# A two-layer kernel whose state-space chunks are computed one pipeline slot further ahead, beside a feed-forward network

## What is computed

```python
# branch 1: state space layer (4 heads of 64, state of 128), 2048 tokens
h   = h * dA_t[:, :, None, None] + dtx_t[..., None] * B_t[:, :, None, :]   # per token, a scan
y_t = einsum('bhpn,bhn->bhp', h, C_t)
y   = (y + D * xh) * silu(z);   out = residual + einsum('bli,di->bld', y, out_proj_w)
# branch 2: feed-forward network of ternary weights, width 512
h = silu(_tlin(x, w1_w, w1_s)) * _tlin(x, w2_w, w2_s)
h = gelu(_tlin(h, h1_w, h1_s));  h = gelu(_tlin(h, h2_w, h2_s));  out = _tlin(h, w3_w, w3_s)
```

## Time and profile before

| | |
|---|---|
| time of three runs | 628.39 us median (627.77 to 628.84) |
| the profiled execution: its own time | 632.69 us |
| its span of instructions | 630.9 us |
| mean granted clock of PE | 0.984 of full speed |
| busy over the span: PE, PEld, DVE, ACT, POOL | 582.4, 345.5, 371.0, 453.5, 142.8 us |

### The profile page before, as it was taken

How to read it: one execution, slowest core, us unless ns; L and a number is a source line. 1 busy time by engine, 2 the same in 40 slices (tenths; PEclk the granted TensorE clock), 3 DMA queues, 4 the chain that set the end, 5 groups by cost and what they waited for, 6 DMA issues and landing times.

```text
span 630.9 us, 11320 instructions
## 1 busy us (share of the span) xinstructions
PE 582.4 (92%) x4048; PEld 345.5 (55%) x4053; DVE 371.0 (59%) x1022; ACT 453.5 (72%) x602; POOL 142.8 (23%) x171
## 2 busy tenths in 40 slices
PE   4669999999999999999897899799989999999998
PEld 4324334444343333333334477478767888888887
DVE  7884765646444353475516765683276676676753
ACT  2368988999989999989666275555766576566663
POOL 2043222020110011002700745103003131222231
PEclk9878999999999999999989999999999999999999
DMA  7112002013422220210317220200000000000000
GB/s 229 29 34 68 2 1 68 1 41 105 169 96 92 101 85 1 69 68 9 109 26 224 67 73 39 80 2 0 0 1 1 2 18 0 1 18 1 2 17 18
DMA packets 31175, 31.00 MB, mean 49 GB/s; under 512 B 6912, under 2 KB 21024, under 8 KB 31120
## 3 DMA queue, kind: packets, MB, share of 16 engines
q1 hardware_dynamic: 29872, 27.71, 14.0%
q0 software_dynamic: 1248, 2.57, 1.1%
HBM read 13.44 MB, written 12.89 MB: 42 GB/s over the span
## 4 chain that ended last, share of the span: by engine, by line
PE 64%; DVE 19%; ACT 7%; issue 5%; POOL 2%; SPq 1%; DMA 1%; DVEq 0%; POOLq 0%; ACTq 0%
PE ps L1311 18%; PE ps L1292 9%; PE ps L92 4%; PE ps L94 4%; PE ps L93 4%; PE ps L1622 2%; PE ps L1388 2%; PE ps L1375 2%; DVE r L2449 1%; PE ps L1488 1%; PE ps L1204 1%; DVE r L2388 1%; ACT r L958 1%; DVE r L2385 1%; SPq L706 1%
## 5 line engine op out<-in xcount | busy, mean ns | idle before, releaser
L958 ACT ACTIVATE r<-ps 128x1024 f32<-128x1024 f32 x272 | 258.4, 1034 | 34.2 <-PE ps L1292 31.7
L1311 PE MATMUL ps<-r 128*32 128x512 f32 (+3 forms) x1280 | 147.9, 549 | 2.2 <-DVE r L2043 1.0
L835 POOL TENSOR_SCALAR_AFFINE_SELECT r<-r 128x512 f32<-128x512 f32 (+1 forms) x80 | 47.8, 602 | 218.7 <-ACT r L958 218.4
L1292 PE MATMUL ps<-r2r 32*128 32x512 f32 (+3 forms) x640 | 79.3, 452 | 8.1 <-DMA r2r<-r2r 4.3
L1292 PEld LDWEIGHTS ps<-r2r 32*128 32x128 f32 x640 | 34.8, 186 | 51.4 <-ACT r L958 20.8
L873 POOL TENSOR_TENSOR r<-r 128x512 f32<-128x512 f32 x16 | 23.1, 1446 | 139.0 <-ACT r L1129 139.0
L1311 PEld LDWEIGHTS ps<-r 128*32 128x32 f32 x1280 | 28.0, 109 | 42.7 <-issue 30.3
L94 PE MATMUL ps<-r2r 128*128 128x512 f32 x112 | 44.3, 395 | 0.0
L93 PE MATMUL ps<-r2r 128*128 128x512 f32 (+1 forms) x96 | 35.8, 372 | 0.0
L813 POOL DMA_INDIRECT rows_by_expert<-r x16 | 17.8, 1110 | 63.2 <-DVE r L1958 59.4
L1129 ACT ACTIVATE r<-r 128x512 f32<-128x512 f32 x16 | 10.1, 633 | 28.7 <-DVE r L2449 28.7
(11 more groups left out here) (405 smaller groups left out, 1208.5 us busy)
## 6 DMA issues: line engine op xcount, KB each, us to landing
rows_by_expert<-r SPq DMA_DIRECT2D x34, 258.0 KB, 2.5
r2r<-r2r SPq DMA_DIRECT2D x60, 64.0 KB, 2.0
r<-in_f_W SPq DMA_DIRECT2D x1, 2048.0 KB, 9.3
r<-rows_by_expert SPq DMA_DIRECT2D x23, 64.5 KB, 1.8
res<-in_x SPq DMA_DIRECT2D x4, 256.0 KB, 4.1
r<-in_g_h1T SPq DMA_DIRECT2D x1, 1024.0 KB, 5.7
r<-in_g_h2T SPq DMA_DIRECT2D x1, 1024.0 KB, 7.9
r<-rows_by_token SPq DMA_DIRECT2D x4, 256.0 KB, 3.9
```

Source lines behind the costliest of these rows:

```text
L835: pool.affine_select(blk, blk, pattern, ALU.is_ge, nothing, base=0, channel_multiplier=-1).then_inc(s_msk, 1)
L958: act.activation(probs[:, n % PBUFS, :, :], ps[:, b:b + 2, :], ACT.Exp).then_inc(s_exp, 1)
L1292: m = pe.matmul(ps[:, 2 * (n % SBUFS) + h, at:at + TB - query], kst[32 * j:32 * j + 32, group, P * kt:P * kt + P], qst[32 * j:32 * j + 32, ...
L1311: m = pe.matmul(ps[32 * j:32 * j + 32, 6, query:TB], vp[:, kt, group, :], probs[:, (2 * v + j // 2) % PBUFS, j % 2, at:at + TB - query], s ...
```

## The change

`chunk(i + 1)` on PE moves from the odd slot, behind `state(i)`, to the even slot 2i, behind `projected(i - 1)` and ahead of `state(i)`. On DVE `chunk_started(i + 1)` moves from the even slot 2i + 2 to the odd slot 2i + 1, behind that slot's low half and `chunk_added`; `weighted` stays in the even slot, behind `state_carried`. On ACT the exponentials move from ahead of the gelu of the even slot to behind the gelu (and behind the tanh) of the odd slot before it. A semaphore `s_cb` counts `dtx`, the last reader of the product bank on DVE, and stands in for two waits: PE's on the operands of DVE ahead of `chunk(i)`, and DVE's on its own steps in `weighted`. The work itself, its sizes and its instructions are the same.

```diff
@@ ACT
                 for o in range(FO):
                     if o == 0:
                         gated_high(b, FO - 1)
-                    if o % 2 == 0:
-                        decays(SLOT(b, o) // 2)
+                        if not b:
+                            decays(0)
                     middle_gelu(b, o)
+                    if o % 2:
+                        decays(SLOT(b, o) // 2 + 1)
                 for o in range(FO):
                     if o and b < NB - 1:
                         gated_high(b + 1, o - 1)
-                    if o % 2 == 0:
-                        decays(SLOT(b, FO + o) // 2)
                     last_gelu(b, o)
                     if b < NB - 1:
                         up_tanh(b + 1, o)
+                    if o % 2 and SLOT(b, FO + o) // 2 + 1 < NCH:
+                        decays(SLOT(b, FO + o) // 2 + 1)
@@ PE
             def chunk(i):
                 if i:
-                    pe.wait_ge(s_cx, 2 * i)
+                    pe.wait_ge(s_cb, i)
                     pe.wait_ge(s_ce, 2 * i)
...
             def chunk_units(s):
                 if s % 2:
                     state(s // 2)
+                else:
+                    if s:
+                        projected(s // 2 - 1)
                     if s // 2 + 1 < NCH:
                         chunk(s // 2 + 1)
-                elif s:
-                    projected(s // 2 - 1)
@@ DVE
-                step.mark(dve.tensor_tensor(dtx[:, b], ps[:, 0, P:P + DI].rearrange("p (h d) -> p h d", h=NH),
-                                            over(dt_f[:, NH * i:NH * i + NH], PD), ALU.mult))
+                dve.tensor_tensor(dtx[:, b], ps[:, 0, P:P + DI].rearrange("p (h d) -> p h d", h=NH),
+                                  over(dt_f[:, NH * i:NH * i + NH], PD), ALU.mult).then_inc(s_cb, 1)
             def weighted(i):
                 b = i % 2
-                step.settle()
+                dve.wait_ge(s_cb, i + 1)
...
-                    if s % 2:
+                    if s == 0:
+                        chunk_started(0)
+                        weighted(0)
+                    elif s % 2 == 0:
+                        state_carried(s // 2 - 1)
+                        weighted(s // 2)
+                        if o == 0:
+                            down_added(b - 1)
+                    else:
                         if s >= 3:
                             chunk_added(s // 2 - 1)
                         if o == 1 and b:
                             finished(b - 1)
-                    elif o == 0:
-                        chunk_started(s // 2)
-                        if b:
-                            state_carried(s // 2 - 1)
-                        weighted(s // 2)
-                        if b:
-                            down_added(b - 1)
-                    else:
-                        state_carried(s // 2 - 1)
-                        chunk_started(s // 2)
-                        weighted(s // 2)
+                        if s // 2 + 1 < NCH:
+                            chunk_started(s // 2 + 1)
                     if o >= FO and b < NB - 1:
                         up_gated(b + 1, o - FO)
```

More of the change, by code:

```diff
@@ L456, in build @@
         s_cx = sem("chunk_operands_from_dve")
+        s_cb = sem("chunk_products_read_by_dve")
         s_cy = sem("chunk_outputs")
```

## The result

The changed kernel takes 631.77 us (median of 8 runs, 630.73 to 634.19) where the kernel before took 627.74 (8 runs, 625.96 to 628.84). The ratio is 1.0071, with a 95% interval of 1.0049 to 1.0093: slower by 4.5 us (0.0071 of 627.7; the two medians by themselves lie 4.0 us apart), where +4.4 was forecast.

A forecast was written before the change was run, and what follows sets the result against it. PE, busy throughout the stage, was taken to bound the kernel. Terms +5.3 (slots 8b + 6), -1.1 (waits for POOL), +0.1 (first block) and +0.15 (slot 30) gave +4.4 on 628.4, so 632.8 us; range 628.0 to 634.8.

The forecast's parts named there:

- `projected` in slots 6, 14 and 22: Third last slot of three blocks: PE waits for DVE's L2481, delayed by the late high half and POOL; 1.76 us each.
- The unhindered part: Slots 6, 14, 22: PE's wait from the late high half if POOL does not hold DVE; 0.48 us each.
- The held part: Same slots: POOL's running instructions hold DVE's `gated_low` and L2469, so the stall is 1.76 us instead of 0.48.
- The waits of `state` for POOL, -1.1 us: PE's `state` waiting for POOL's `cs` outside slot 3; these waits go, -1.1 us, bounds 0.9 and 1.3.
- The first block, +0.1: `projected(0)` starts 1.27 us later, 1.06 us of `state(1)`'s wait returns in slot 3; net taken as +0.1.
- Slots 8b + 2: With b from 1: no stall, PE arriving 0.1 us after L2481 ends; taken as 0, bounds 0 and +3.6 us.
- Slot 30: L2481 runs into POOL's last `mm` and makes PE wait some 0.15 us.
- B: Rival: high half late, but DVE gets through beside POOL wholly or partly; +0.5 to +3 us, chance 0.18.
- C: Rival: the 0.1 us margin in slots 8b + 2 fails; 636.4 us if in all three, chance 0.07.
- F: Rival: 1.38 us drain at ACT's table switch lengthens the three stalls, 4.1 us in all; 636.9 us, chance 0.03.
- D: Rival: faster, `gated_low` is free in time and only waits for POOL go; 626.3 to 627.5 us, chance 0.12.
- E: Rival: change does nothing, what it removes and makes late is hidden under PE's queue; 628.4 us, chance 0.08.

The follow-up runs named there:

- Experiment 1: Changed kernel with ACT's order of before: high half ahead of the exponentials again in odd last slots; 631.59 us, ratio 0.9983 to the kernel before.
- experiments 2 and 3: Changed kernel, chunks 3, 7, 11: POOL held until the previous gated output (633.67 us, ratio 1.0018); POOL's two products cut to 2 of 128 columns (632.33 us, 1.0017).
- experiment 4: Changed kernel plus two small DVE products ahead of `gm` in chunks 5, 9 and 13; one execution 637.27 us, stage 3.72 us above the changed kernel.
- experiment 6: Changed kernel with ACT's order of before and POOL held in every chunk until the previous gated output; 632.09 us, ratio 0.9993 to the kernel before.
- experiment 5: Only PE's part of the change, `chunk` one slot earlier, with DVE and ACT in their order of before; 637.70 us, ratio 1.0183 to the kernel before.

## Why the prediction was right

The median moved as forecast (+4.5 us by the ratio, +4.4 forecast), and the stage by +4.85. Term by term, by the starts of PE:

- *`projected` in slots 6, 14 and 22.* Forecast 1.76 us each; measured 1.75, 1.74, 1.74. Experiment 1 shows that the place of the high half is what makes it, experiments 2 and 3 that the port adds 1.36 of it. The unhindered part was set at 0.48 and is 0.39: the high half follows `ec` after 0.47 us and not 0.54. The held part was therefore 0.08 larger than worked out. That the two errors cancel is not luck: once `gated_low` is held, it leaves when POOL's first product ends (534.86, 4.05 us after the tanh began; 4.03 was worked out), whenever the high half came.
- *The waits of `state` for POOL, -1.1 us.* They are gone: every distance ahead of `state` is at its usual 0.33 or below. They had been 0.38, 0.27, 0.27 and 0.16 us over it, 1.08 in all.
- *The first block, +0.1.* L1668 was to start 1.52 us late; it was 1.39. Net of the wait that went in slot 3 the block lost 0.16.
- *Slots 8b + 2.* No wait, as forecast, and by the 0.14 us that experiment 4 used up. PE came to the projection of slot 10 at 515.59, 0.24 us after L2485 had ended, where 0.1 had been worked out.
- *Slot 30.* 0.34 in place of 0.23 between starts: 0.11 us, forecast 0.15.
- *A term that was missing.* After each stall the projection itself is slower:

```profile
480.86 0.61 PE L1668 MATMUL ps<-r 128*128 128x128 f32 x4
481.31 0.28 PE L1640 MATMUL ps<-r 128*128 128x128 f32 x1
...
493.75 0.71 PE L1668 MATMUL ps<-r 128*128 128x128 f32 x4 [1.58 <-DVE r L2485]
494.29 0.28 PE L1640 MATMUL ps<-r 128*128 128x128 f32 x1
```

Without a wait its four matmuls take 0.45 us to the next start, behind a stall 0.54: some 0.1 us more. This comes anew in slots 6, 14, 22 and 30 (behind a wait of 0.11 us too); in slot 2 the projection stood behind a short wait before as well and was as slow. With 0.4 us for these four the terms are 5.23 - 1.08 + 0.16 + 0.11 + 0.4 = 4.8 of the 4.85 us. Experiment 1, which undoes three of the stalls, agrees: 5.23 us of waits and three times 0.1 are 5.5 of its 5.57. Why the first matmuls behind a wait are slower is not shown; the granted clock is 1.00 throughout.

Of the rivals, B (no lock) is what experiments 2 and 3 show, +0.8, so the lock was worth 4.06 us in all. C failed to happen by 0.14 us. F, the 1.38 us of drain that the page "ScalarE: Activation LUTs" of the Trainium skill (section "What ACT_TABLE_LOAD costs") adds to a load, did not happen: the exponential started 1.30 us after the start of its load (531.51 to 532.81), with an activation of another table right ahead. D and E fell with the waits themselves.

## What to carry to other kernels

An engine's order is not changed by moving one instruction, but by every instruction that it is moved past. Here "exponentials behind the gelu" left all of ACT's order as it was except for two copies in each of three blocks, and one of these was the head of the chain that PE needs next. Write down both orders of each queue and compare them; what changed places is the change. Then look at who else uses a port or a bank at the new time: the late copy alone cost 0.39 us a slot, the POOL instruction that it now ran into 1.36. And where two engines come to the same port within a tenth or two of a microsecond of each other, as in experiment 4, an order pinned with a semaphore, as in experiment 6, takes away the risk.

## What the runs showed of the hardware

- DVE with two inputs in SBUF and a running POOL `tensor_tensor` exclude each other, and they take turns: between POOL's two instructions, issued back to back, one waiting DVE instruction goes through (L2440 in slot 14), and the next DVE instruction waits for the whole of the second. That turn made 1.10 us of L2473's 1.52. This is as in the earlier trace rows, but for another pair of instructions. DVE steps with one input in the accumulator memory were not held beside a running POOL (0.60 and 0.42 us in slot 16 of the kernel before).
- Four waits of PE of 1.39 to 1.75 us did not lower its clock in the changed kernel: it is 1.00 in all windows of the stage. In experiment 5, though, the windows from 466 us on read:

```profile
466.00:469.50 3.50, 1.88 (x13) 1.42 (x12) 3.26 (x8) 2.11 (x3) 1.42 (x2) 0.98 0.00 0
469.50:473.00 3.50, 3.50 (x10) 2.78 (x10) 1.02 (x3) 1.61 (x3) 1.26 (x1) 0.54 0.02 5
473.00:480.00 7.00, 7.00 (x44) 5.57 (x43) 4.28 (x13) 3.87 (x6) 0.53 (x1) 1.00 0.00 0
```

Behind the wait of 1.73 us in slot 2 eight matmuls, 469.42 to 472.80, ran at the lower of the two levels, 1.2 GHz, with starts 0.43 us apart in place of 0.23. That cost some 1.5 us (3.38 us in place of eight times 0.23). The three later waits of 1.45 us had no such sequel, nor had those of 1.75 us in the changed kernel. What makes the difference, these runs don't settle.
